# First attention pass of a four-layer graph network: score sums of four chunks in one instruction, and three steps of the softmax chain later in the round

## The reference, cut to what matters

```python
aw_q_edge = q_att[etype, col_idx]
msg_edge = v_msg[etype, row_idx]
attn_score = jnp.sum(aw_q_edge * k[row_idx], axis=-1)
score = attn_score * (relation_pri[etype] / SQRT_DK)
m = jax.ops.segment_max(score, col_idx, num_segments=n)
ex = jnp.exp(score - m[col_idx])
denom = jax.ops.segment_sum(ex, col_idx, num_segments=n)
alpha = ex / denom[col_idx]
agg = jax.ops.segment_sum(alpha[..., None] * msg_edge, col_idx, num_segments=n)
```

## Time and profile before

| | us |
|---|---|
| median of 3 runs | 3477.73 (3476.02 to 3478.45) |
| the profiled execution | 3477.75 |
| its span | 3475.9 |
| busy in it: TensorE matmul | 2882.9 |
| busy: VectorE | 2560.1 |
| busy: GpSimd | 2183.1 |
| busy: ScalarE | 1946.9 |

### The profile page before, as it was taken

One profiled execution on the slowest core, in us unless ns is written; L12 is line 12 of the kernel. 1 busy time (PEld: TensorE's weight loads), 2 busy tenths in 40 slices (PEclk: granted clock), 3 DMA queues, 4 the chain that ended last, 5 costly groups with the idle time before them and its releaser, 6 DMA issues. The chain is left out here.

```text
span 3475.9 us, 60577 instructions
## 1 busy us (share of the span) xinstructions
PE 2882.9 (83%) x15683; PEld 1831.2 (53%) x15683; DVE 2560.1 (74%) x6632; ACT 1946.9 (56%) x6316; POOL 2183.1 (63%) x2289
## 2 busy tenths in 40 slices
PE   5799799999987995777777767799999897887885
PEld 4666455555565553555555534577777653333332
DVE  8899889999977554888888843799999874444444
ACT  0478655555531452777777832588888753333333
POOL 1777667777756533666666445777777314777774
PEclk9999889999998997999999889799999996556555
DMA  6334478888841878777767544877777444333334
GB/s 180 97 104 127 139 248 264 262 262 263 262 114 38 275 318 334 248 210 212 208 199 204 134 159 173 233 227 225 229 226 226 130 182 170 102 103 103 103 103 104
DMA packets 260813, 651.81 MB, mean 188 GB/s; under 512 B 66813, under 2 KB 115658, under 8 KB 253706
## 3 DMA queue, kind: packets, MB, share of 16 engines
q0 software_dynamic: 141840, 474.50, 45.6%
q1 hardware_dynamic: 118650, 173.44, 15.6%
HBM read 505.78 MB, written 145.27 MB: 187 GB/s over the span
## 5 line engine op out<-in xcount | busy, mean ns | idle before, releaser
L2114 POOL DMA_INDIRECT a_rows<-table,met x568 | 557.4, 981 | 261.7 <-issue 135.4
L3690 PE MATMUL ps<-rows_in,hot_w 128*128 128x256 f32 x832 | 446.3, 646 | 100.7 <-ACT hot_w L3652 60.8
L1330 POOL DMA_INDIRECT rows_in<-table,met x416 | 412.6, 992 | 148.3 <-issue 85.2
L3640 POOL DMA_INDIRECT rows_in<-table,met x416 | 405.8, 976 | 144.2 <-issue 117.7
L3715 DVE TENSOR_TENSOR xs<-xs,ps 128x256 f32 x416 | 175.1, 421 | 304.1 <-PE ps L3690 300.4
L3690 PEld LDWEIGHTS ps<-rows_in,hot_w 128*128 128x128 f32 x832 | 197.0, 291 | 350.0 <-ACT hot_w L3652 183.8
L3652 ACT ACTIVATE hot_w<-hot,met 128x128 f32<-128x128 f32 x416 | 166.7, 401 | 373.7 <-PE ps L3690 340.2
L2114 POOL DMA_INDIRECT xs<-table,met x264 | 260.5, 987 | 115.7 <-issue 62.0
L2590 PE MATMUL ps<-a_rows,a_hot 128*128 128x260 f32 x1136 | 317.3, 403 | 17.9 <-DVE acc L2596 12.1
L833 POOL DMA_INDIRECT records<-rec,rows x241 | 260.3, 1080 | 88.9 <-issue 72.5
L2596 DVE TENSOR_TENSOR acc<-acc,ps 128x520 f32 x416 | 287.1, 690 | 35.3 <-PE ps L2590 14.4
(11 more groups left out here) (487 smaller groups left out, 6466.7 us busy)
## 6 DMA issues: line engine op xcount, KB each, us to landing
a_hot_t<-one_hots SPq DMA_DIRECT2D x104, 256.0 KB, 4.9
table<-stage SPq DMA_DIRECT2D x25, 1024.0 KB, 3.9
rows_in<-table,met POOLq DMA_INDIRECT x832, 3.7
dst_row<-slot_rows SPq DMA_DIRECT2D x52, 256.0 KB, 5.1
one_hots<-hot_t SPq DMA_DIRECT2D x52, 256.0 KB
by_dst<-dst_rows SPq DMA_DIRECT2D x25, 512.0 KB, 5.7
by_dst<-lo_rows SPq DMA_DIRECT2D x24, 512.0 KB, 4.7
a_rows<-table,met POOLq DMA_INDIRECT x568, 3.8
```

What stands on the lines that cost most here:

```text
L1330: e.indirect_dma_start(self.rows[:, n % self.RING, 0:2 * D], None, self.table, bass.IndirectOffsetOnAxis(ap=self.b.met[:, n, R_SRC:R_SRC + ...
L2114: e.indirect_dma_start(self.row(n, 0, self.width), None, self.table, bass.IndirectOffsetOnAxis(ap=b.met[:, n, self.word:self.word + 1], ax ...
L3640: e.indirect_dma_start(self.rows[:, n % self.RING, :], None, self.table, bass.IndirectOffsetOnAxis(ap=self.b.met[:, n, R_REL:R_REL + 1], a ...
L3690: e.matmul(b.ps[:, n % self.BANKS, 0:D], self.hot_w[:, n % GRP_H, :], self.rows[:, n % self.RING, :], start=True, stop=True).then_inc(self ...
```

## The change

In `Attend1` the product of a pair of chunks goes to one of four buffers, and only the second pair of two is followed by a reduce, over both pairs (128x1024 to 128x16), so four reduces per round take the place of eight. The turn of the scores goes from step 6 to 7 of TensorE's queue, behind sum 6 and the fetch of pair 0. The turn back of the maxima goes from 13 to 15, behind sum 14 and the fetch of pair 3, and VectorE's `below` from 14 to 15, behind add 12. On ScalarE the copies of the turned one-hot matrices go from steps 2, 6, 10, 14 to 3, 7, 11, 15, the row `other` from 10 to 13, and the factor and exponentials from 14 to 15. `Attend2` gets the same names with its old values.

```diff
-                if n % GRP_H == 2 and 0 <= n // GRP_H + 1 < NCH // GRP_H:
+                if n % GRP_H == self.HOT_AT and 0 <= n // GRP_H + 1 < NCH // GRP_H:
                     hot_rows(n // GRP_H + 1)
-                if w < NW and i == self.CHAIN["ends_in"][0] + 2:
+                if w < NW and i == self.OTHER_AT:
...
-                if w < NW and i == WIN - 2:
+                if w < NW and i == self.EXPS_AT:
...
-    TURNS = {"score": 6, "ends": 9, "spread": 12, "back": 13}
+    TURNS, HOT_AT, OTHER_AT, EXPS_AT = {"score": 7, "ends": 9, "spread": 12, "back": 15}, 3, 13, 15
     CHAIN = {"run": (7, True), "most": (8, False), "ends_in": (8, True), "carry": (10, False), "lead": (10, True), "tail": (11, False),
-             "through": (11, True), "picked": (12, True), "most_1": (13, False), "fall": (13, True), "below": (14, False)}
+             "through": (11, True), "picked": (12, True), "most_1": (13, False), "fall": (13, True), "below": (15, False)}
...
-        self.prod = b.sb("a1_prod", [P, 2, 2, D], F32, own)
+        self.prod = b.sb("a1_prod", [P, 4, 2, D], F32, own)
...
     def scored_by(self, w):
-        return (w + 1) * (WIN // 2)
+        return (w + 1) * (WIN // 4)
...
-        if pair >= 2:
-            e.wait_ge(self.scored, pair - 1)
+        if pair >= 4:
+            e.wait_ge(self.scored, pair // 2 - 1)
         e.wait_ge(self.fetched, self.fetched_by(n + 2))
-        e.tensor_tensor(self.prod[:, pair % 2, :, :], b.ps[:, pair % 2, :].rearrange("p (c f) -> p c f", c=2),
+        e.tensor_tensor(self.prod[:, pair % 4, :, :], b.ps[:, pair % 2, :].rearrange("p (c f) -> p c f", c=2),
                         self.rows(s, 2)[:, :, 0:D], ALU.mult).then_inc(self.product, 1)
+        if j % 2 == 0:
+            return
         e.wait_ge(self.product, pair + 1)
-        if j == 0 and w >= 2:
+        if j == 1 and w >= 2:
             e.wait_ge(self.chain, self.chained(w - 2, "below"))
-        e.tensor_reduce(self.score[:, w % 2, 2 * j * H1:2 * (j + 1) * H1],
-                        self.prod[:, pair % 2, :, :].rearrange("p c (h f) -> p (c h) f", h=H1), AX_X, ALU.add).then_inc(self.scored, 1)
+        e.tensor_reduce(self.score[:, w % 2, 2 * (j - 1) * H1:2 * (j + 1) * H1],
+                        self.prod[:, pair % 4 - 1:pair % 4 + 1, :, :].rearrange("p a c (h f) -> p (a c h) f", h=H1), AX_X, ALU.add
+                        ).then_inc(self.scored, 1)
```

More of the change, by code:

```diff
@@ L2517 @@
     FETCHES = {8 + k: [(1, k)] for k in range(WIN // 2)}
-    TURNS = {"score": 3, "ends": 7, "spread": 10, "back": 13}
+    TURNS, HOT_AT, OTHER_AT, EXPS_AT = {"score": 3, "ends": 7, "spread": 10, "back": 13}, 2, 8, 14
     CHAIN = {"run": (4, True), "most": (5, True), "ends_in": (6, True), "carry": (8, False), "lead": (8, True), "tail": (9, False),
```

## The result

The changed kernel takes 3491.47 us (median of 6 runs, 3481.32 to 3496.29) against 3476.88 for the kernel before on the same chip (6 runs, 3472.50 to 3478.45): ratio 1.0042, 95% interval 1.0033 to 1.0052. It is slower by 14.6 us, where 3465 and "faster" were forecast. The time lies above the range.

What follows compares the result with a forecast made beforehand. VectorE's own in-order queue was taken to bound the first attention pass. Terms -0.72 - 0.49 - 0.48 + 1.09 = -0.60 us a round; with low clock counted, 0.51 less than 23.93, 12.7 us over some 25 rounds: 3465, range 3450 to 3484.

Steps and rivals of the forecast that it cites:

- The reduces: VectorE: half the reduces, each over four chunks, save 0.72 us a round at full clock (bounds 0.24 to 0.80).
- `score` at 7: TensorE's turn of the scores one step later removes VectorE's wait ahead of add 7: 0.49 us a round saved.
- The register load: VectorE: product 4 has no reduce, so the load ahead of the rescale is hidden: 0.48 us a round saved.
- `back` at 15: TensorE's turn of the maxima queues behind sum 14 and a fetch; VectorE waits 1.39 us at `below`, costing 1.09 a round.
- part 5: ScalarE's one-hot copies, `other` and exponentials a step later: cost and gain 0, with over 4 us a round to spare.
- Which clock: TensorE's clock falls behind the 2.1 us stand ahead of sum 14; 0.6 of 0.92 us counted, 23.42 us a round.
- the last line of step 4: Upper bound at `below`: at 1.2 GHz sum 14 and the fetch add 0.42 and 0.50 us, stall 2.31, at most 2.63.
- B: Rival: TensorE keeps the full clock, 22.87 us a round, kernel 3451 us; chance 0.17.
- C: Rival: the wait at `below` replaces what is removed, clock down each round, 23.79 us a round, kernel 3474; chance 0.17.
- D: Rival, slower: VectorE stalls 2.63 us at `below` and the register load (0.48) isn't hidden, kernel 3494; chance 0.11.
- E: Rival: VectorE's lone products save nothing, 0.48 us back, 23.90 us a round, kernel 3477; chance 0.08.
- own signs of error: Wrong if `below` waits much less than 1.3 us, the rescale keeps 1.08, or `run` waits for the scores' turn.

Runs made afterwards that it cites:

- the filled kernel: The changed kernel plus 14 spare matmuls between TensorE's sum 13 and sum 14: 3452.31 us, ratio 0.9936 to the kernel before; on a slower chip 1.0086.
- the moves alone: The changed kernel's moved steps with the two-chunk reduces of the kernel before: 3503.26 us, ratio 1.0075 to the kernel before; on a slower chip 1.0001.
- the reduces alone: The kernel before with only the reduces made over four chunks, all steps unmoved: 3473.07 us, ratio 0.9997; on a slower chip 1.0020.

## Why the prediction was wrong

Right, by its own steps:

1. The reduces. The long one takes 1.22 us, as worked out; the lone product has 0.59 to 0.60 to the next instruction. The Trainium skill, "VectorE: DVE Perf Modes", "The DRAIN you can't avoid", says that a semaphore between two operations costs nothing extra and so spoke against more than 0.24 here; this case's rows go against it a second time (0.60 against 0.72 where VectorE waits for its own product). The same section says that a next operation that isn't held starts earlier, which the prediction left out and which the 0.60 agrees with.
2. `score` at 7. The wait ahead of add 7 is gone.
3. The register load is hidden ahead of the rescale.
4. `back` at 15, at full clock. `below` follows add 12 by 1.58 us with the turn behind sum 14 and by 0.34 with the turn ahead of it, a stall of 1.24 where 1.39 was forecast. The sum of all parts, 22.87, was measured as 22.66 in the filled kernel, and the moves alone as 24.12 for 24.07. Between these two the reduces with the hidden load are worth 1.46, and 1.20 was counted. Most of the other 0.26 can be read from the two timelines: with the moves alone `run` starts 0.49 us after add 5 in the round that I compared, in the filled kernel 0.34 (with two-chunk reduces the turn of the scores seems to come a little late), and from the rescale to the next instruction it takes 0.12 against 0.07. The 22.66 is 0.21 under the sum mainly since add 7 follows `open_hot` by 0.20 (0.27 counted), that second step is 0.05 shorter, and add 13 follows add 11 by 2.41 (2.45 counted).

Not shown either way is part 5, the ScalarE moves at 0: on a comparable chip they weren't measured by themselves.

What failed is "Which clock", and with it the last line of step 4. The prediction saw the stand of 2.1 us, took it that the clock falls behind it, and priced that at 0.92 us at most, sum 14 and the fetch, of which it counted 0.6 (0.55 us). In the profiled execution the low clock costs 24.46 - 22.66 = **1.80 us** a round, over three times as much (22.66 is one of the shortest rounds of the filled kernel; its 15 wholly at full clock take 22.79 on average). By VectorE's timeline over the 24 rounds it lies in two places:

- `below` waits 46.5 us in all, 1.94 a round, 0.79 over the 1.15 of full clock. This is the place that was forecast, and within its bound.
- Adds 0 and 1 of the next round. Add 1 waits 1.81 to 2.19 us in nine rounds (18.9 us) and 0.90 in one, add 0 some 0.4 in eight (3.3 us): 23.1 us, **0.96 a round**, none of which was in the sum or in its bounds. At full clock add 1 waits 0.21 anyway, so 0.88 of it is the low clock's.

22.66 + 0.79 + 0.88 = 24.33, and 24.46 was measured; 0.07 more are five waits of 0.27 to 0.45 ahead of adds 7, 9, 10, 12 and 13 that the filled kernel has in the same rounds too. Against the forecast's 23.42 the second place is 0.88 of the 1.04 that are missing; the first adds 0.24 (0.79 for 0.55) and the 0.13 left over is more than made up by the full-clock sum (22.66 for 22.87).

The second place was missed since the price was read from the stretch of 3.4 us behind `back` and from the two sums and the fetch in it. In the kernel before, the turn is the first thing behind the stand, and most of what follows it at 1.2 GHz is hidden: its rounds lose only 0.47 (23.93 against 23.46). But the low stretch was also taken to last 3.4 us, as behind `back` before, and in the changed kernel it doesn't always. In the 24 rounds before, 17 low stretches of 3.4 us begin and none longer. Of those that begin in the 24 rounds of the changed kernel eleven last 3.4 us, one 6.8 and nine 10.2. The nine rounds in which add 1 waits 1.81 us or more are exactly those that start inside a long one: eight in one of 10.2 us, and the first in one that has lasted since before the pass. So the low clock covers the end of a round and the start of the next. There TensorE has sum 15, two rescale factors, sum 0, four transposes, a fetch and sum 1 in a row, and VectorE, made faster by steps 1 to 3, reaches add 1 before them. What decides between a short and a long stretch is not shown by any run.

One round of the kernel before already showed both, and neither the prediction nor its rows has it: in the first of the 24, of 25.22 us, the clock is low for 10.2 us over the start of the round, and add 1 waits 1.95 us.

```profile
1395.16:1405.38 10.22, 8.85 (x35) 5.95 (x36) 7.07 (x18) 7.98 (x28) 7.78 (x9) 0.50 0.92 305
```

```profile
1404.64 0.42 DVE L2502 TENSOR_TENSOR acc<-acc,ps 128x260 f32 x1 [1.95 <-PE ps L2499]
```

How many rounds pay it varies: nine in the profiled execution (24.46 a round), 14 in the one taken later (24.89). The spread of the runs, 15 us, fits that, though only these two have a profile.

The rivals. B was the state of the kernel that keeps its clock, and the filled kernel met its number, but the changed kernel doesn't keep it. C had the clock down in every round and stopped at the same bound, 23.79. D was nearest in time, 3494, but that is mostly luck: its stall of 2.63 was reached in one round (2.75; 2.40 in five), its load was hidden, and half of the loss lies where no rival looked. E is refuted by the 0.60 above.

The prediction's own signs of error didn't fire: the waits that it named, the reduce and the rescale came out as it said. What did miss was its mix of rounds of 22.9 and 23.8: they run from 23.42 to 26.28. It had no line for the adds behind the next rescale. That the profile's first line of stretches would show a lower mean clock was not said either, and it is the one number that points at the cause.

## What to carry to other kernels

When a change lengthens a stand of TensorE, don't price the low clock by the step behind the stand: take the length of the low stretches from every round that has one, the odd ones too, list what stands in its queue until the clock is back, and look up which wait of another engine each ends, across the round's border too. Put the step that another engine waits for first behind the stand, and see whether spare matmuls in the stand pay (27 us on `back` at 14, some 39 us on `back` at 15, there from ratios on two chips); with one of two stands filled the low clock came at the other here. A saving on the engine that leads the ring can turn into longer stands of the others and be taken back there in full, as with the reduces alone (0.9997).

## What the runs showed of the hardware

- Work that nothing reads made a kernel faster: 3418.59 against 3445.10 with 12 spare matmuls a round (1.47 us of TensorE each round), and 3452.31 against 3491 to 3493 with 14 (not on the same chip; ratios 0.9936 against 1.0042 and 1.0047).
- Low stretches of the clock come in different lengths in one kernel: 3.4 us (1634.08 to 1637.48 before), 6.8 and 10.2 (1804.86 to 1815.08 in the changed kernel), always at 0.50.
- Whether the clock falls is not a matter of one stand alone: with the stand ahead of `back` filled in the kernel before, it fell behind the stand for the scores in seven rounds of 24, where it costs more.
- Chips differ by 12 to 13%: the same kernel takes 3474 to 3477 us on some and 3896 to 3938 on others, and an edit that gains 23 us on the one (ratio 0.9936) loses on the other (1.0086). In the filled kernel on the slower chip VectorE stands 2.75 us ahead of `a_carry` in one round that I read, 2.6 us after the matmul that it needs has ended, and a round takes 27.7 us on average in place of 23.2. The cause stays open.
